# A vision block with a quantised feed-forward on one core: DVE's step in another order, and one column more for ACT

## The reference

```python
x = x + conv(ln_c(x)) + ln_c(x)          # depthwise 3x3 conv, 'SAME'; ln over the 96 channels, eps 1e-6
t = tokens(x)                            # 32 * 112 * 112 tokens of 96
h = relu(qlinear(ln_t(t), W1, b1))       # 96 -> 384, ln over the 96 channels, eps 1e-5
t = t + qlinear(h, W2, b2)               # 384 -> 96
# qlinear(x, W, b) = q_acc(q_acc(q_mul(x) @ q_mul(W).T) + q_mul(b))
# q_mul rounds to 5 exponent and 2 mantissa bits (float8e5), q_acc to 5 and 10 (float16)
```

## Time and profile before

| | |
|---|---|
| median of 3 runs | 4024.47 us (4016.77 to 4032.15) |
| the profiled execution | 4024.61 us |
| its span (first to last instruction) | 4022.9 us |
| busy: DVE / PE / ACT / POOL | 3613.3 / 3152.2 / 2935.4 / 1720.4 us |
| granted clock of PE, mean | 0.966 |
| moved by DMA | 714.6 MB, 178 GB/s |

### The profile page before, as it was taken

One profiled execution on the slowest core, in us unless ns is written; L12 is line 12 of the kernel. 1 busy time (PEld: TensorE's weight loads), 2 busy tenths in 40 slices (PEclk: granted clock), 3 DMA queues, 4 the chain that ended last, 5 costly groups with the idle time before them and its releaser, 6 DMA issues.

```text
span 4022.9 us, 87017 instructions
## 1 busy us (share of the span) xinstructions
PE 3152.2 (78%) x24678; PEld 2482.8 (62%) x24678; DVE 3613.3 (90%) x12635; ACT 2935.4 (73%) x6204; POOL 1720.4 (43%) x915
## 2 busy tenths in 40 slices
PE   3088888878888788888888888888888888889977
PEld 2077666666666666666666666666666666667744
DVE  4647999999999999999999999998999999999998
ACT  3456777777777777777777777777777777777765
POOL 0002444444444444444444444444444444445555
PEclk9999999999999999999999999999999999999955
DMA  4466666666666666666666666666666666665533
GB/s 146 114 170 172 188 188 185 187 184 187 187 185 189 177 190 190 182 180 185 188 185 188 185 186 188 185 188 183 187 189 186 188 185 196 191 191 172 160 106 94
DMA packets 277321, 714.60 MB, mean 178 GB/s; under 512 B 34777, under 2 KB 34882, under 8 KB 276802
## 3 DMA queue, kind: packets, MB, share of 16 engines
q1 hardware_dynamic: 276802, 708.57, 60.1%
HBM read 539.84 MB, written 168.59 MB: 176 GB/s over the span
## 4 chain that ended last, share of the span: by engine, by line
PE 55%; ACT 31%; issue 7%; DMA 5%; DVE 1%; ACTq 1%; SPq 0%; POOLq 0%; POOL 0%; DVEq 0%
PE conv_ps L384 33%; ACT images L465 14%; PE hid_ps L352 13%; ACT hid L444 9%; PE y_ps L365 7%; ACT xt L436 4%; ACT y L452 4%; DMA band_ring<-bands 2%; DMA xn<-in_x 2%; ACTq L167 1%; DMA bands<-images 1%; PE conv_ps L326 1%; DVE stats L582 0%; PE y_ps L326 0%; PE xt_ps L339 0%
## 5 line engine op out<-in xcount | busy, mean ns | idle before, releaser
L384 PE MATMUL conv_ps<-images,band_ring 112*112 112x222 f32 (+1 forms) x9216 | 2064.9, 363 | 604.9 <-ACT xt L436 385.2
L384 PEld LDWEIGHTS conv_ps<-images,band_ring 112*112 112x112 f32 x9216 | 1568.0, 179 | 896.7 <-issue 656.7
L444 ACT ACTIVATE hid<-hid_ps 128x896 f16<-128x896 f32 x1344 | 1226.3, 913 | 505.2 <-PE hid_ps L352 505.2
L224 POOL TENSOR_TENSOR xf<-xf,images 112x768 f32<-112x768 f32 x448 | 980.3, 2188 | 1299.2 <-DVE hid L571 893.7
L230 POOL TENSOR_TENSOR xf<-xf,y 112x768 f32<-112x768 f32 x448 | 736.8, 1645 | 999.3 <-DVE y L602 997.7
L626 DVE SCALAR_TENSOR_TENSOR xq<-xf,stats,xt_ps 112x96 fp8e5<-112x96 f32 x3584 | 844.3, 310 | 0.0
L365 PE MATMUL y_ps<-w2t,hid 128*128 128x96 f16 x10752 | 634.5, 211 | 173.8 <-ACT y L452 172.3
L365 PEld LDWEIGHTS y_ps<-w2t,hid 128*128 128x128 f16 x10752 | 555.1, 100 | 329.0 <-ACT y L452 213.3
L465 ACT ACTIVATE images<-xn,neg_mean,rstd 112x96 f32<-112x96 f32 x1792 | 723.0, 545 | 13.2 <-DVE neg_mean L618 13.2
L352 PE MATMUL hid_ps<-xt,w1t 96*128 96x448 fp8e5 x2688 | 695.6, 369 | 27.7 <-ACT xt L436 19.5
L452 ACT ACTIVATE y<-y_ps 112x384 f16<-112x384 f32 x896 | 443.8, 495 | 364.4 <-PE y_ps L365 362.9
(11 more groups left out here) (46 smaller groups left out, 571.1 us busy)
## 6 DMA issues: line engine op xcount, KB each, us to landing
band_ring<-bands SPq DMA_DIRECT2D x768, 294.0 KB, 5.2
xn<-in_x SPq DMA_DIRECT2D x448, 336.0 KB, 3.5
xf<-in_x SPq DMA_DIRECT2D x448, 336.0 KB, 4.8
out<-xf SPq DMA_DIRECT2D x448, 336.0 KB, 3.9
bands<-images SPq DMA_DIRECT2D x2, 7056.0 KB, 24.5
xf<-in_L_ffn_W SPq DMA_DIRECT2D x2, 144.0 KB, 2.8
xf<-in_L_conv_kernel SPq DMA_DIRECT2D x3, 3.4 KB
xf<-in_L_ffn_b SPq DMA_DIRECT2D x1, 42.0 KB, 3.4
```

The lines of the kernel that those rows point to most:

```text
L224: pool.tensor_tensor(x2, x2, images[:, b, i, :, cols].rearrange("p c w -> p w c"), ALU.add).then_inc(with_conv, 1)
L384: mm = pe.matmul(dst[:, :, lo:hi], band_ring[:, n % BAND_RING, PAIR * dx + i, :], images[:, m % 2, :, ch, lo + dx - 1:hi + dx - 1], start= ...
L444: nc.scalar.activation(hid[:, c % 2, TOK * j:TOK * (j + 1)].rearrange("p (u n) -> p u n", u=2), hid_ps[:, k, :, 0:HALF * H], ACT.Identity) ...
```

## The change

DVE's step gets another order. Before: the third bias of the chunk before, statistics, quantise, reciprocals, y bias, scaling of the next chunk, columns, two biases of the same chunk. After: statistics, the scaling (of the chunk of this step, with the reciprocals of the step before), all three biases of the chunk before, quantise, reciprocals, y bias, columns. ACT's square roots stand at the head of its step, and it takes five columns in place of four. POOL adds first `y` (one step later than before, chunk c-3), after it has waited for DVE's columns of the step before, then the convolution; it no longer waits for the biases.

```diff
-ACT_COLS = 4
+ACT_COLS = 5
...
-                def add_conv(r, c, t):
+                def add_conv(r, c):
...
-                    if ffn_in(t - 1):
-                        wait(pool, hid_biased, J * (LOOP * r + c - FFN_AT))
                     pool.wait_ge(xf_in[e % FFN_RING], dma_count(r, e, FFN_RING))
...
-                def add_ffn(r, c):
-                    e = c - FFN_AT
+                def add_ffn(r, c, t):
+                    e = c - 3 - FFN_AT
+                    if norm_in(t - 1):
+                        wait(pool, normed[1], LOOP * r + c - NORM_AT)
                     wait(pool, y_biased, LOOP * r + e + 1)
                     res = xf[0:H, e % FFN_RING]
-                    pool.tensor_tensor(res, res, y[:, c % 2], ALU.add).then_inc(summed, CW)
+                    pool.tensor_tensor(res, res, y[:, e % 2], ALU.add).then_inc(summed, CW)
 
                 def step(r, c, t):
+                    if ffn_in(t - 3):
+                        add_ffn(r, c, t)
                     if ffn_in(t + 2):
-                        add_conv(r, c, t)
-                    if ffn_in(t - 2):
-                        add_ffn(r, c - 2)
+                        add_conv(r, c)
...
                 def step(r, c, t):                       # ACT
                     now, before, norm = ffn_in(t), ffn_in(t - 1), norm_in(t)
+                    if ffn_in(t + 1) or norm:
+                        deviation(r, c, t)
                     if now:
                         copy_xt(r, c)
                     save_conv(r, c - 1, t - 1, 3, C)
                     if now:
                         cast_hid(r, c, 0)
-                    if ffn_in(t + 1) or norm:
-                        deviation(r, c, t)
...
                 def scale(r, c):
-                    e = c + 1 - FFN_AT
+                    e = c - FFN_AT
                     for w in range(CW):
                         op = dve.scalar_tensor_tensor(
-                            out=xq_8[:, (c + 1) % 2, w // 2, 0:C, w % 2], in0=xf[0:H, e % FFN_RING, w, :],
-                            scalar=stats[:, c % 2, 0, w, 1:2], in1=rstd_t[:, w:w + 1].broadcast_to([H, C]),
+                            out=xq_8[:, c % 2, w // 2, 0:C, w % 2], in0=xf[0:H, e % FFN_RING, w, :],
+                            scalar=stats[:, (c - 1) % 2, 0, w, 1:2], in1=rstd_t[:, w:w + 1].broadcast_to([H, C]),
...
                 def step(r, c, t):                       # DVE
-                    if before:
-                        add_bias(r, c - 1, 2)
                     if after or norm:
                         statistics(r, c, t)
+                    if now:
+                        scale(r, c)
                     if before:
+                        for j in range(J):
+                            add_bias(r, c - 1, j)
                         quantise(r, c - 1)
                     if after or norm:
                         invert(r, c, t)
                     if ffn_in(t - 2):
                         add_y_bias(r, c - 2)
-                    if after:
-                        scale(r, c)
                     if norm:
                         normalise(r, c)
-                    if now:
-                        add_bias(r, c, 0)
-                        add_bias(r, c, 1)
```

More of the change, by code:

```diff
@@ L218, in add_conv @@
                         wait(pool, conv_saved, GROUPS * (2 * r + e // UNIT + 1))
-                    if ffn_in(t - 1):
-                        wait(pool, hid_biased, J * (LOOP * r + c - FFN_AT))
                     pool.wait_ge(xf_in[e % FFN_RING], dma_count(r, e, FFN_RING))
                     x2 = xf[0:H, e % FFN_RING]
-                    pool.tensor_tensor(x2, x2, images[:, b, i, :, cols].rearrange("p c w -> p w c"), ALU.add).then_inc(with_conv, 1)
-                def add_ffn(r, c):
-                    e = c - FFN_AT
+                    pool.tensor_tensor(x2, x2, images[:, b, i, :, cols].rearrange("p c w -> p w c"),
+                                       ALU.add).then_inc(with_conv, 1)
+                def add_ffn(r, c, t):
+                    e = c - 3 - FFN_AT
+                    if norm_in(t - 1):
+                        wait(pool, normed[1], LOOP * r + c - NORM_AT)
                     wait(pool, y_biased, LOOP * r + e + 1)
                     res = xf[0:H, e % FFN_RING]
-                    pool.tensor_tensor(res, res, y[:, c % 2], ALU.add).then_inc(summed, CW)
+                    pool.tensor_tensor(res, res, y[:, e % 2], ALU.add).then_inc(summed, CW)
                 def step(r, c, t):
+                    if ffn_in(t - 3):
+                        add_ffn(r, c, t)
                     if ffn_in(t + 2):
-                        add_conv(r, c, t)
-                    if ffn_in(t - 2):
-                        add_ffn(r, c - 2)
+                        add_conv(r, c)
                 run(pool, step)
```

## The result

The changed kernel takes 4689.12 us (median of 4, 4684.06 to 4787.09) against 4020.62 for the kernel before beside it: a ratio of 1.1657, interval 1.1629 to 1.1686. It is slower, as forecast, but by 16.6% and not by 7.5%: the time lies far above the range. The profiled execution took 4689.85 us, 665 more than the one before. The ratio leaves out the fourth execution (4787.09 us at a mean clock of 0.873, the other three 0.891 to 0.892). Of the 302 us that I had foreseen the 292 of the ring are there; some 360 are not in my forecast, but in a rival to which I gave 3%.

What follows compares the result with a forecast made beforehand. The prediction took a PE-ACT ring as the bound, not DVE. 390 steps x (0.39 + 0.36) = 292 us, plus 11 and 7, less 8, gave +302: 4325 us from 4024.6; its own range 4285 to 4360, 8 in 10 4260 to 4390.

Steps and rivals of the forecast that it cites:

- 302 us: Whole kernel: total growth forecast, +292 for the main stage, +11 and +7 for other stages, -8 for irregular steps.
- the ring: PE and ACT hand one chunk back and forth between copies of xt: 8.32 us a step before, 9.07 forecast after.
- The terms 0.39 and 0.36: On ACT, per step: 0.39 us for the square roots at the step's head, 0.36 us for the fifth column.
- The reordering at nothing: DVE's new order, scaling one step later: cost and gain 0, since the ring does not pass through DVE.
- slack of 1.7 us: PE's transposes end at about 7.4 us, the next copy of xt is due at 9.07: later scaling leaves 1.7 us.
- the timetable in the prediction: Times of DVE's work, loads and PE's transposes after the copy of xt, with a period of 9.07 us.
- The sum for the stage, 390 x 0.75 = 292 us: 390 steps with second layer and normalisation, each longer by 0.39 + 0.36 us on the ring: 292 us.
- PE's part of the ring, 4.55 us: PE's first to last ring pieces, matmuls of channel, first layer, convolution and second layer, run from 2011.51 to 2016.06.
- rival (d): PE's longer idle lowers its clock to 0.90; its ring part grows 0.9 us, 350 us more, 4675; chance 0.03.
- only to about 1.5: PE's idle before the convolution, 1.07 us a time, was to grow to about 1.5; the argument against the lower clock.

Runs made afterwards that it cites:

- split_norm: Kernel before with two of ACT's four normalised columns moved in front of the first cast of y; 3803.28 us, ratio 0.9461.
- ring_plus: Kernel before with three small ACT operations, whose results nobody reads, in front of each copy of xt; 4945.87 us, ratio 1.2297.
- before_cols5: Kernel before with five normalised columns on ACT in place of four and nothing else; 4303.87 us, ratio 1.0717.
- the filling: Six or eight unused PE matmuls where PE waits for the copy of xt, added to the changed kernel; 4409.06 us (six), 4441.65 us (eight).
- cols4: Changed kernel with four columns on ACT again in place of five; 4263.54 us, ratio 1.061.
- std_behind_copy: Changed kernel with ACT's square roots moved directly behind the copy of xt, five columns kept; 4399.16 us, ratio 1.0963.

## Why the prediction was wrong

- **That PE and ACT form the ring and DVE is off it: right.** It gave both edits of ACT their sign. split_norm shows it from the other side: no instruction less on any engine, 217 us gained.
- **The terms 0.39 and 0.36: right** (the trace after has 0.38 for the square roots and 0.36 for the column). 9.07 us were forecast and measured. (The range of the forecast, 4285 to 4360, is narrower than the bounds named for it, which add up to 4273 to 4374; the measured time is far outside both.)
- **The reordering at nothing: right in the changed kernel**, whose undisturbed steps are the ring's, and only there. The bound was stated as slack of 1.7 us; the condition (a ring of 9 us) was not. PE did come to wait for xq, 178.5 us in mid run, which the timetable in the prediction doesn't have; this is off the ring, since ACT waited only 2.8 us there for PE's transposes. On a ring of 8.33 the reordering costs 129 us, most of which the earlier loads and the other order of the statistics take away.
- **The sum for the stage, 390 x 0.75 = 292 us: the step that failed.** It took PE's part of the ring, 4.55 us, as a constant. After, the stretch with that part took 4.65 us at a clock of 1.00 and 7.82 at 0.59, and the clock over mid run is 0.90: (10.07 - 8.39 - 0.75) x 390 = 363 us, and 292 + 363 = 655 of the 665. What failed was not overlooked but misjudged: rival (d) had the mechanism, the clock of 0.90, the 0.9 us a step and 4675 us, 14 off the measured time, and I gave it 0.03. That its numbers fit so well is luck: 0.90 was the clock of another stretch of the kernel before, 300 to 350, and ring_plus, with the same ring, has 0.84. My argument against it was that PE's idle before the convolution grows "only to about 1.5" us from 1.07. That number was near: 365.4 us in 218 waits, 1.68 a time. But a gap of that kind, taken alone, does not tell the clock: 1.44 us went with 1.00 before, and 1.36 with the fall after. What grew with the ring is the whole stretch between the first cast of y and the restart, 3.67 to 4.42 us with as little work in it as before (the filling lies in the gap, so it does not part the two); and the kernel before was itself not far from the edge: 0.36 us more of ring (before_cols5) already bring its clock in mid run from 0.99 to 0.95.
- **The rule that the engine with the highest occupancy is to be optimised first** (the Trainium skill, Perfetto Trace Analysis, section Identifying the Most-Contended Engine) had DVE at 90%. The change gave DVE less to wait for, and the kernel got slower; moving two columns within ACT's step gained 5.4% with DVE's instructions untouched. Here the rule misled and the chain was right. It holds once the ring is short: in split_norm DVE is busy 94% and is the bound.

Open is what, at one ring length, sets how often the clock falls. ring_plus and the changed kernel both have 9.07 us and 0.84 and 0.90; cols4 and std_behind_copy have 8.7 and 0.97 and 0.92. The changed kernel's PE idles partly before the transposes and partly before the restart, ring_plus's almost all in one piece, but cols4 against std_behind_copy does not show which feature decides.

## What to carry to other kernels

Where the chain goes back and forth between two engines, add up one turn from start to start; a term on it costs its full length and one in its idle costs nothing, whatever the busy shares say. If TensorE is on that ring, time added on the other engine is also time in which TensorE is lightly used: look at the granted clock beside its busy share in neighbouring stretches, and price the sum at both levels before giving either a small chance. An operation that must stay on an engine may cost nothing if it is put where that engine already waits, as long as the wait is long enough in every kind of step.

## What the runs showed of the hardware

The granted clock fell with no single idle of PE above 1.36 us just before it, in a stretch where PE was in use for 1.87 of 4.47 us; in the kernel before it stayed at 1.00 over an idle of 1.44, in a stretch with 1.69 of 3.67 us in use. The same 34 matmuls took 4.65 us at 1.00 and 7.82 at 0.59. Unused matmuls in the light stretch brought the clock in mid run from 0.84 to 0.99 and the time from 4945.87 to 4377.21 us. A bias of DVE that takes 0.44 us by itself took 2.23 us when it started inside an addition of POOL's.
